# The output bias of the attention: from bias matmuls on TensorE to an addition in place on GpSimd

## What is computed

```python
h = concat([cls, patches(x) @ W.T + b] + pos_enc, txt)      # 64 x 114 x 256
n = layernorm(h)
Q, K, V = n @ Wq.T + bq, n @ Wk.T + bk, n @ Wv.T + bv
Q, K = elu(Q) + 1, elu(K) + 1
KV, K_sum = K^T V (per head), sum of K over the tokens
att = Q KV / (Q K_sum + 1e-6)
h = h + (att @ Wo.T + bo)                                   # bo: 256 numbers, the bias of this case
n = layernorm(h)
h = h + expert[argmax(n @ gate_w.T)](n, gated by sigmoid)   # one of 8 experts for each token
```

## Time and profile before

| | us |
|---|---|
| median of 3 runs | 570.28 |
| lowest, highest | 568.74, 573.35 |
| span of the profiled execution, first to last instruction | 532.9 |
| PE busy in the span | 478.5 (90%) |
| DVE busy | 394.3 (74%) |
| POOL busy | 348.1 (65%) |
| ACT busy | 335.1 (63%) |

### The profile page before, as it was taken

How to read it: one execution, slowest core, us unless ns; L and a number is a source line. 1 busy time by engine, 2 the same in 40 slices (tenths; PEclk the granted TensorE clock), 3 DMA queues, 4 the chain that set the end, 5 groups by cost and what they waited for, 6 DMA issues and landing times. The chain is left out here.

```text
span 532.9 us, 13968 instructions
## 1 busy us (share of the span) xinstructions
PE 478.5 (90%) x3686; PEld 445.1 (84%) x3687; DVE 394.3 (74%) x1324; ACT 335.1 (63%) x805; POOL 348.1 (65%) x727
## 2 busy tenths in 40 slices
PE   4999899999999999999999999999954499999991
PEld 4988789999898999989999988888843498989990
DVE  4666478888887888788878877877854288888881
ACT  4334467667666757766676776766632488888870
POOL 0463234677777677777777778887776067877774
PEclk9999899999999999999999999999995599999996
DMA  8951000111121112711111211110013567852220
GB/s 298 281 168 34 14 23 14 39 35 33 34 56 33 30 37 81 238 30 51 39 30 36 55 31 31 42 35 22 18 38 99 155 196 220 241 160 82 78 79 31
DMA packets 31578, 43.24 MB, mean 81 GB/s; under 512 B 8541, under 2 KB 23840, under 8 KB 31539
## 3 DMA queue, kind: packets, MB, share of 16 engines
q1 hardware_dynamic: 21650, 27.12, 17.4%
q0 software_dynamic: 9216, 15.12, 8.9%
q10 hardware_dynamic: 672, 0.53, 0.3%
HBM read 26.45 MB, written 17.17 MB: 82 GB/s over the span
## 5 line engine op out<-in xcount | busy, mean ns | idle before, releaser
L521 POOL DMA_INDIRECT sorted_rows<-rows,place x64 | 75.1, 1174 | 39.7 <-POOL place L516 28.7
L608 POOL DMA_INDIRECT out<-result,result_id x64 | 62.6, 978 | 30.2 <-DVE result L1059 13.7
L684 ACT ACTIVATE k_neg<-k_in 114x512 f32<-114x512 f32 x32 | 20.3, 634 | 59.7 <-DVE k_in L961 59.7
L1078 PE MATMUL b_kvp<-wkv_hi,xnT_hi 128*114 128x512 f32 x128 | 52.9, 413 | 0.0
L696 ACT ACTIVATE xn<-rows_all,shift,rstd 114x256 f32<-114x256 f32 (+1 forms) x64 | 34.9, 593 | 27.6 <-issue 24.2
L498 POOL TENSOR_TENSOR rstd<-ve,half_neg 114x2 f32<-114x2 f32 x64 | 47.0, 734 | 5.3
L1079 PE MATMUL b_kvp<-wkv_lo,xnT_hi 128*114 128x512 f32 x128 | 50.4, 394 | 0.0
L1080 PE MATMUL b_kvp<-wkv_hi,xnT_lo 128*114 128x512 f32 x128 | 50.2, 392 | 0.0
L495 POOL TENSOR_SCALAR ve<-mv 114x2 f32<-114x2 f32 x64 | 15.3, 239 | 53.2 <-DVE mv L840 29.3
L550 POOL TENSOR_TENSOR k_sb<-k_exp,k_relu 114x512 f32<-114x512 f32 x32 | 41.2, 1287 | 5.8 <-issue 4.4
L1078 PE MATMUL b_kvp<-wgu_hi,xsT_hi 128*128 x128 | 37.7, 294 | 6.3 <-DVE xsT_lo L778 6.3
(11 more groups left out here) (174 smaller groups left out, 1771.3 us busy)
## 6 DMA issues: line engine op xcount, KB each, us to landing
rows_all<-sorted_rows SPq DMA_DIRECT2D x64, 130.0 KB
rows_all<-in_x SPq DMA_DIRECT2D x16, 432.0 KB, 4.8
rows_all<-in_txt SPq DMA_DIRECT2D x32, 154.0 KB
rows_all<-in_wgu SPq DMA_DIRECT2D x8, 256.0 KB, 4.5
sorted_rows<-rows,place POOLq DMA_INDIRECT x64, 3.7
rows_all<-in_wdown SPq DMA_DIRECT2D x8, 128.0 KB, 4.7
out<-result,result_id POOLq DMA_INDIRECT x64
rows_all<-in_w_tok SPq DMA_DIRECT2D x2, 384.0 KB, 4.1
```

The source lines that it names most:

```text
L521: G.indirect_dma_start(out=scratch[0:EXPERTS * REGION, :], out_offset=bass.IndirectOffsetOnAxis(ap=place[:, k, b:b + 1], axis=0), in_=rows ...
L608: G.indirect_dma_start(out=out, out_offset=bass.IndirectOffsetOnAxis(ap=result_id[:, k:k + 1], axis=0), in_=result[:, k, :], in_offset=Non ...
L1078: T.matmul(to, left_hi, right_hi, start=start, stop=False)
```

## The change

The two bias matmuls of each pair and the whole preparation of `bias3` go. The bias is loaded as a tile `bo_s` of 114 x 256 (one DMA that repeats the row on 114 partitions, in place of the DMA of one row). In each POOL step, behind the addition that makes `k_sb`, POOL adds `bo_s` to the two images' rows of pair i-1 in `rows_all`, in place, once the first normalisation of that pair (`xn_ready`) has read them. DVE's residual then waits for this too (`biased`).

```diff
-        bias3 = sb("bias3", [P, D], BF16)
+        bo_s = sb("bo_s", [TOK, D])
...
-            sp.dma_start(bias_row[:], bo).then_inc(s_weights, 16)
+            sp.dma_start(bo_s[:], bo.to_broadcast([TOK, D])).then_inc(s_weights, 16)
...
                     G.tensor_tensor(k_sb[:], k_exp[:], k_relu[:], ALU.add).then_inc(k_ready, 1)
+                if (i - 1).within(PAIRS):
+                    p = i - 1
+                    until = ahead(pool, p.upto())
+                    pool.wait_ge(s_prep, 1)
+                    pool.wait_ge(xn_ready, until)
+                    rows_p = rows_all[0:TOK, bass.ds(2 * p.n, 2), 0:D]
+                    G.tensor_tensor(rows_p, rows_p, bo_s[:].rearrange("p (a d) -> p a d", a=1).to_broadcast([TOK, 2, D]),
+                                    ALU.add).then_inc(biased, 1)
...
-            left = bias_row
-            for r in range(3):
-                G.tensor_copy(bias_part[:, r, :], left[:]).then_inc(s_bias_chain, 1)
-                if r < 2:
-                    pool.wait_ge(s_bias_chain, 2 * r + 1)
-                    G.tensor_tensor(bias_left[:], left[:], bias_part[:, r, :], ALU.subtract).then_inc(s_bias_chain, 1)
-                    pool.wait_ge(s_bias_chain, 2 * r + 2)
-                left = bias_left
...
-                act.wait_ge(s_bias_chain, 5)
-                for r in range(3):
-                    act.dma_start(bias3[r:r + 1, :], bias_part[:, r, :]).then_inc(s_bias_dma, 16)
...
                 dve.wait_ge(wo_done, p.upto())
+                dve.wait_ge(biased, p.upto())
...
-                dve.wait_ge(s_bias_dma, 48)
...
-                        T.matmul(to, ones_bf[:, :], bias3[:, :], start=True, stop=False)
                         for c in range(KC):
...
-                                           False, c == KC - 1)
+                                           c == 0, c == KC - 1)
...
-            pe.wait_ge(s_bias_dma, 48)
```

More of the change, by code:

```diff
@@ L173, in build @@
             w_tok_hi, w_tok_lo = parts("w_tok", [P, FC, D], room)
-            bias_row = sb("bias_row", [1, D], at=room)
-            bias_left = sb("bias_left", [1, D], at=room)
-            bias_part = sb("bias_part", [1, 3, D], BF16, room)
         with ExitStack() as room:
@@ L262, in build @@
         s_expert_w = sem("s_expert_w")
-        s_bias_dma = sem("s_bias_dma")
         s_prep = sem("s_prep")
         s_posb = sem("s_posb")
-        s_bias_chain = sem("s_bias_chain")
+        biased = sem("biased")
         w_hi = sem("w_hi")
@@ L729, in w_tok_part, with small_loads @@
                 S.copy(w_tok_hi[:, half].rearrange("p f d -> p (f d)"), w_tok_raw[:, at]).then_inc(w_hi, 1)
-            def bias_rows():
-                act.wait_ge(s_bias_chain, 5)
-                for r in range(3):
-                    act.dma_start(bias3[r:r + 1, :], bias_part[:, r, :]).then_inc(s_bias_dma, 16)
+            def small_loads():
                 act.wait_ge(s_small, 16 * SMALL_DMAS)
@@ L739, in _ @@
                 lambda: w_tok_part(0, s_tokw), 0, lambda: w_tok_part(1, s_tokw2), 1,
-                2, 3, "steady", lambda: step(Turn(0, -3)), 12, bias_rows, 13,
+                2, 3, "steady", lambda: step(Turn(0, -3)), 12, small_loads, 13,
                 14, lambda: step(Turn(0, -2)), 15, lambda: step(Turn(0, -1))])
@@ L782, in _ @@
             V.memset(half_neg[:], -0.5)
-            V.memset(ones_bf[:], 1.0)
-            V.memset(bias3[:], 0.0).then_inc(s_prep, 1)
+            V.memset(ones_bf[:], 1.0).then_inc(s_prep, 1)
             def w_tok_part(h):
```

## The result

The change makes the kernel slower. On the chip of the first comparison the kernel before took 569.6 us (median) and the changed one 587.1 us: ratio 1.033, with a 95% interval of 1.026 to 1.040. The forecast was 596.6 us, in a range of 583 to 606. Direction and mechanism came out; the size was 17.5 us, not 26.3. Every ratio here compares only the executions that lie within 1.5% of their kernel's fastest.

What follows compares the result with a forecast made beforehand. The prediction took PE to bound steps 5 to 23, with POOL 0.5 us behind and becoming the bound. Its terms, 17.7 + 0.9 + 5.6 + 1.4 + 1.4 - 0.7, gave +26.3 us: 596.6 us, range 583 to 606.

Steps and rivals of the forecast that it cites:

- POOL becomes the bound: Stage A, steps 5 to 23: POOL alone would need 11.36 us a step against 10.43, +17.7 us over 19 steps.
- The price of the addition: POOL, each step: the addition taken as 1.29 us like `k_sb` plus a 0.11 us gap, 1.40 us.
- The 9.96 us: POOL's own time for a step without the addition, read from one loop step of before that has no wait.
- The stall behind qT: POOL's small instruction held while DVE's `qT` runs: about 0.45 us in each step, counted within the 9.96 and 11.11.
- rival A: POOL's steps: `qT` falls in the gap or itself waits, POOL regains 0.45 us a step; 584 us, chance 0.15.
- The present period is PE's: Steps 5 to 23 before: PE sets the 10.43 us period, POOL stands 0.5 us behind; two matmuls cost 0.23 us.
- rival C: POOL's gap ahead of the scatter shrinks, the addition is hidden and PE's saving counts: -7.4 us, 563 us; chance 0.04.
- the 0.7 us of steps 1 to 4: Start of stage A: additions hidden in POOL's waits, PE's three first pairs save 0.23 us each, -0.7 us.
- Steps 29 to 31 and the drain: End of stage A: three additions of 4.20 us less 2.84 us of waits, +1.4 us; drain (step 32) +1.4 us.
- The first stage: Ahead of stage A: removing the bias split gains nothing, the larger bias load costs nothing, at worst 1 us.
- Span and time: Whole kernel: the +26.3 us added alike to the profiled span of 532.9 us and the median of 570.28 us.
- Rival D: Stage A: PE, idle 1.2 to 2.4 us per step, falls to a lower clock; 620 us or more, chance 0.04.

## Why the prediction was right, and where it wasn't

**POOL becomes the bound: right.** The step of the argument that carried the sign was that steps 25 to 28 of the kernel before are already the experiment: one more 512-wide instruction, no wait left, a longer step. The changed kernel's steps 5 to 23 look like those, and the kernel with both additions and matmuls shows that nothing of PE's is in the loss.

**The price of the addition: 1.24, not 1.40 us.** The addition takes 1.27 us, as `k_sb` does. From `k_sb` to the addition POOL needs 1.24 us, and from the addition to `ve` 1.35, where from `k_sb` to `ve` it was 1.35 to 1.43 in steps 25 to 28 before. So the gap that I added once more was already paid. In steps 25 to 28 the measured +4.5 us is 3 x 1.24 and one step of 11.9. Over the 19 steps this term was 19 x 0.16 = 3.0 us too large. The 9.96 us beside it was a little too large as well: its step has 1.43 us from `k_sb` to `ve`, where 1.35 is enough, and 19 x 0.08 is 1.5 us.

**The stall behind qT: half of rival A.** I took it for a part of every step, because it is in the one wait-free step that I read the earlier trace rows. It was missing in 8 of 19 steps, in which `rstd` started some 0.1 us ahead of `qT`: 8 x 0.46 = 3.7 us. The three terms make 17.7 into 9.5; measured were 10.0. Rival A's mechanism was named right, its all-or-nothing form was not, and the stall went neither of the two ways that it gave.

**"The present period is PE's": wrong.** This was read from a busy share of 99.7%. Taking the matmuls out gave 0.06 us a step, not 0.23, and a reordering on POOL gave 0.22. What the runs show in its place is a path that runs through POOL; that it is the loop over four engines is the best account of it, with PE and POOL close behind (10.3 and 10 us of 10.4). It cost the forecast little, as the matmuls were costed at nothing wherever POOL sets the pace. But rival C's 563 us rested on it, and so did the 0.7 us of steps 1 to 4. These can't be told from the traces: step 5 began 1.1 us earlier in the first profile of the changed kernel and 0.35 us later in the second.

**Steps 29 to 31 and the drain:** +1.9 and +1.25 us for +1.4 and +1.4, right within half a microsecond in this profile. In the first profile of the changed kernel steps 29 to 31 took 34.85 us, +3.5; see the clock below.

**The first stage: at nothing, right within 0.4 us.** Without the bias split POOL's wait for `mv` grew from 6.97 us to 11.84.

```profile
43.27 0.87 POOL L491 TENSOR_SCALAR ve<-mv 114x2 f32<-114x2 f32 x1 [11.84 <-DVE mv L831]
```

**Span and time: wrong.** The 37.4 us were read as a fixed cost. That the sum could be added to 570.28 even so was luck: on both chips on which the changed kernel was timed it costs about the same (17.5 and 17.8 us).

**Rival D, the clock:** it does fall. In steps 25 to 28 it costs nothing that can be seen, in step 30 it may cost up to 2 us. It is told below.

## What to carry to other kernels

An engine that is busy to 100% needn't be the bound: take one thing off it, or see whether a stretch with extra work elsewhere gets longer, before counting a gain there. The slack of the engine that receives the work is its wait per step, not what its busy share leaves: here some 0.8 of 10.4 us at 74% busy (2.16 us from `k_sb` to `ve` on the mean, and 1.35 where there is no wait). So half of the addition was free in steps 5 to 23 and the whole was not. And where an instruction of one engine holds up another engine, as `qT` does POOL, each stall becomes part of the period as soon as the engine that is held is the bound.

## What the runs showed of the hardware that I had not expected

**The clock of PE falls in the middle of stage A.** The granted clock in four windows of steps 25 to 28 of the changed kernel:

```profile
325.00:330.00 5.00, 3.03 (x30) 2.76 (x28) 2.38 (x12) 2.20 (x6) 4.67 (x9) 1.00 0.15 46
330.00:335.00 5.00, 5.00 (x27) 4.56 (x27) 3.42 (x10) 3.64 (x10) 3.75 (x11) 0.66 0.00 0
...
350.00:355.00 5.00, 3.05 (x29) 2.78 (x27) 2.33 (x12) 2.21 (x6) 4.67 (x9) 1.00 0.12 37
355.00:360.00 5.00, 5.00 (x26) 4.70 (x26) 3.04 (x8) 2.94 (x8) 3.48 (x11) 0.66 0.02 5
```

In every second step, after a window in which PE was busy only 3.0 of 5 us, the next one has a mean clock of 0.66: PE is at 1.2 GHz for most of it and back at 2.4 GHz in the window behind. In the kernel before the clock stays at 1.00 in these steps. PE does 27 instructions in the slow window where it does 40 in a fast one, and then has no idle time. The steps still take POOL's 12.36 us, so the slower clock is hidden by PE's slack.

It may not be hidden everywhere. These are steps 29 and 30, first in the first profile of the changed kernel, then in the second:

```profile
373.58:385.79 12.21, 10.04 (x49) 8.82 (x48) 6.86 (x21) 6.28 (x15) 10.12 (x20) 0.72 0.08 22
385.79:398.41 12.62, 12.42 (x102) 11.59 (x100) 10.09 (x32) 8.13 (x18) 8.51 (x17) 1.00 0.07 18
```

```profile
374.81:387.28 12.47, 10.31 (x64) 9.44 (x63) 8.33 (x25) 7.19 (x17) 10.38 (x20) 0.86 0.08 22
387.28:398.06 10.78, 10.61 (x87) 9.78 (x85) 8.51 (x29) 7.18 (x17) 8.51 (x16) 1.00 0.08 21
```

Where the clock of step 29 is 0.72 and not 0.86, PE does 49 instructions in it and not 64, has 102 to do in step 30, and that step takes 1.8 us more with PE busy nearly all of it. The kernel with both matmuls and addition shows the same (0.72, then a step of 12.86 us). No run tested this apart.

**The same kernel takes 535 us on two chips and 570 on a third.** The profiles differ in stage B: it takes 125 to 128 us on the first two, and on the third 156 us or more in each of four kernels, as in the kernel before with the reordering (407.5 to 563.7). In the first comparison, on a chip that the record doesn't name and on which the kernel before took 569.6 us, it was 158 us in the changed kernel. Stage A of the changed kernel ends within 1 us of the same time there and on one of the first two. What stage B waits for on the slower chips was not tested and stays open. It touches the verdict little: the two comparisons of the changed kernel have ratios of 1.033 and 1.035.
